# Two graph layers on one core: q kept on chip as fp16 pairs, one-hot matrices on DVE, unrolled gathers

## The chip, the cores and the metric

One core of a Trainium2 chip runs the whole program in one launch. The time is device microseconds of that core from start to end of the launch; a kernel's time is the median of its runs. TensorE is called PE, VectorE DVE, ScalarE ACT, GpSimd POOL and SyncE SP.

## The reference, cut to what matters

There are 6250 nodes of 512 features (fp32) and 100000 edges, sorted by destination.

```
# layer 0
h   = relu(layernorm(x))
agg = segment_sum(h[src], dst) / max(deg, 1)
g   = relu(agg @ W_l.T + b_l + h @ W_r.T)
x   = x + batchnorm(g)
# layer 1
h = relu(layernorm(x))
Q, K, V = h @ Wq, h @ Wk, h @ Wv                 # 8 heads of 64
score = exp(clip(sum(K[src] * Q[dst]) / 8, -5, 5))    # per edge and head
wV = segment_sum(V[src] * score, dst);  Z = segment_sum(score, dst)
out = x + batchnorm(h + wV / (Z + 1e-6))
```

## The kernel before, in words

The nodes are cut into 49 windows of 128. The sorted edges are cut into groups of 256 (two halves, G = 2, of 128 edges), and a table lists 440 steps, each one group against one window; a group that crosses a window's border appears in two steps. The tables stay in SBUF: `src_t` (source rows, an out-of-range number where the edge belongs to another window), `rel_t` (destination within the window), and small rows with one value a step: `col_t` (the window's column in `sums`), `par_t`, `new_t` (1 where a window begins), `row_t` and `qcol_t`. Stages follow one another with a barrier between them:

- `prepare` (L111) makes the tables. Its POOL part ends in eight gathers written out one after another (L179 to L183).
- `embed` (L565) makes y = h @ W_l.T for every window, stored as fp16 pairs in DRAM (`y_d`).
- `aggregate` (L829) does the 440 steps of layer 0. POOL gathers y rows of each half (L881, two gathers a step, eight steps of buffers, U = 8) with indices that ACT copies beforehand for pairs of steps from `src_t` into `idx` (L856, "staging", since the loop's step is a register). DVE makes a one-hot matrix of both halves in one instruction (L904). PE multiplies it with the gathered rows (L977).
- `dense` (L267, called with `layer` = 1 only) splits the three weight matrices into a high and a low part (L462 to L468 on ACT, L382 on DVE), and for each window makes Q, K and V with 36 matmuls (L549). K and V go to `kv_d`. Q, divided by 8, is stored as high and low part in fp32 slots to `q_d` (L329, L435, L492).
- `attend` (L1112) does the 440 steps of layer 1, each engine with its own order, several steps apart: PE does in its iteration t `total(t-2)`, `turn(t+2)`, `expand(t+1)`; ACT does `weigh(t-1)`, staging for every second step (L1212, L1213), `copy_hot(t+2)`; DVE does `multiply(t)`, `scale(t-1)`, `reduce(t)`, `one_hot(t+3)` of the second half on even steps only (L1266), a flush where a window ended (L1006, L1017), `clip(t)`. POOL makes the other one-hot halves (L1192: one half on even steps, both on odd ones) and then issues the step's two gathers of K and V rows (L1196, 512 KB each). SP loads the window's q at each new window from `q_d` into four slots (L1170). `expand` multiplies the turned one-hot (`hotT`) with q's two parts (L1341), so every edge has its q row in PSUM.
- the last two stages make batch norm and the output.

Within one engine everything runs in the written order; between engines semaphores count steps.

Of the kernel before, what the change touches and what calls it, by code (L numbers as in the profile page):

```python
# [16 lines left out]
F32 = mybir.dt.float32  # L17
# [14 lines left out]
def build(nc, x, src, dst, W_l, b_l, W_r, gamma0, beta0, Wq, Wk, Wv, gamma1, beta1, out):  # L32
# [21 lines left out]
    QB = 4  # L54
# [8 lines left out]
    q_d = nc.dram_tensor("q_d", (WINDOWS * P, 2 * D), F32).ap()  # L63
# [15 lines left out]
    with life:  # L79
# [4 lines left out]
        row_t = sb(life, "row_t", [1, TS], I16)  # L84
        qcol_t = sb(life, "qcol_t", [1, TS], I16)
# [25 lines left out]
        def prepare():  # L111
            with ExitStack() as ctx:
# [34 lines left out]
                def _(block):  # L147
# [63 lines left out]
                    def _(dve):  # L211
# [23 lines left out]
                        then(nc.vector.tensor_scalar(row_t[:, :], win[:, :], float(P), None, ALU.mult))  # L235
                        then(nc.vector.tensor_copy(win_t[:, :], win[:, :]))
                        then(nc.vector.tensor_copy(qcol_t[:, :], win[:, :]))
                        then(nc.vector.tensor_scalar(par_t[:, :], qcol_t[:, :], 1, None, ALU.bitwise_and))
                        then(nc.vector.tensor_scalar(par_t[:, :], par_t[:, :], float(D), None, ALU.mult))
                        then(nc.vector.memset(zero[:, :].bitcast(F32), 0.0))  # L240
                        then(nc.vector.tensor_scalar(qcol_t[:, :], qcol_t[:, :], QB - 1, None, ALU.bitwise_and))
                        then(nc.vector.tensor_scalar(qcol_t[:, :], qcol_t[:, :], float(2 * D), None, ALU.mult))
# [24 lines left out]
        def dense(layer, given, A_bc=None, C_bc=None):  # L267
# [3 lines left out]
            M = len(given)  # L271
            tag = str(layer)
            with ExitStack() as ctx:
                w_hi = sb(ctx, "w_hi" + tag, [P, M, KC, D], F32R)
                w_lo = sb(ctx, "w_lo" + tag, [P, M, KC, D], F32R)
                x_sb = sb(ctx, "x_sb" + tag, [P, 2, D])
                x1 = sb(ctx, "x1_sb", [P, 2, D]) if layer else x_sb
                h = sb(ctx, "h" + tag, [P, 2, D])
                st = sb(ctx, "st" + tag, [P, 6])
                mv = sb(ctx, "mv" + tag, [P, 2])  # L280
                sd = sb(ctx, "sd" + tag, [P, 1])
                rs = sb(ctx, "rs" + tag, [P, 2])
                nb = sb(ctx, "nb" + tag, [P, 2])
                hT_hi = sb(ctx, "hT_hi" + tag, [P, 2, D], F32R)
                hT_lo = sb(ctx, "hT_lo" + tag, [P, 2, D], F32R)
                o_sb = sb(ctx, "o_sb" + tag, [P, 2, 2, D])
                w_st = [o_sb[:, :, :, :].rearrange("p a b d -> p (a b) d")]
                if layer:
                    q_sb = sb(ctx, "q_sb", [P, 2, 2, D], F32R)
                    w_st.append(q_sb[:, :, :, :].rearrange("p a b d -> p (a b) d").bitcast(F32))  # L290
                else:
                    b_row = sb(ctx, "b_row", [1, D])
                    b_bc = sb(ctx, "b_bc", [P, D])
                ps_t = [pb(ctx, f"ps_t{tag}{k}", [P, 512]) for k in range(2)]
                ps_o = [[pb(ctx, f"ps_o{tag}{k}{j}", [P, 512]) for j in range(M)] for k in range(2)]

                w_in, w_turned, w_high, w_split, b_in = sems("w_in" + tag, M), *(
                    sem(n + tag) for n in ("w_turned", "w_high", "w_split", "b_in"))
                x_in, t_made, t_sum, normal = sems("x_in" + tag, 2), sem("t_made" + tag), sem("t_sum" + tag), sem("normal" + tag)
                var_ready, dev_ready, shift_ready, h_made = (sem(n + tag) for n in ("var_ready", "dev_ready", "shift_ready", "h_made"))  # L300
                q_high = sem("q_high" + tag)
                turned, high, split, made, by_act, by_dve = (
                    sem(n + tag) for n in ("turned", "high", "split", "made", "by_act", "by_dve"))
                kept, stored = sems("kept" + tag, 2), sems("stored" + tag, 2)

                def later(w):

                    return not isinstance(w, int) or w >= 2

                @nc_block()  # L310
                def _(block):
                    @block.sync
                    def _(sp):
                        def load(w, par, n=P):
                            if later(w):
                                sp.wait_ge(t_made if layer else h_made, w - 1)
                            sp.dma_start(x_sb[0:n, par, :], x[ds(w * P, n), :]).then_inc(x_in[par], 16)
# [6 lines left out]
                        def store(w, par):  # L324
                            sp.wait_ge(by_act, w + 1)
                            sp.wait_ge(by_dve, w + 1)
                            rows = ds(w * P, P)
                            if layer:
                                sp.dma_start(q_d[rows, :], q_sb[:, par, :, :].rearrange("p a d -> p (a d)").bitcast(F32)).then_inc(stored[par], 16)  # L329
                                sp.dma_start(kv_d[rows, :], o_sb[:, par, :, :].rearrange("p a d -> p (a d)")).then_inc(stored[par], 16)  # L330
                            else:
                                sp.dma_start(y_d[rows, :], o_sb[:, par, 0, :]).then_inc(stored[par], 16)
                                sp.dma_start(z_d[rows, :], o_sb[:, par, 1, :]).then_inc(stored[par], 16)

                        def both(w, par, n=P):
                            load(w + 3, 1 - par, n)
                            if layer:
                                keep(w + 1, 1 - par)
# [1223 lines left out]
```

## Time and profile before

| | us |
|---|---|
| median of 3 runs | 3829.07 (3824.32 to 3831.52) |
| the profiled execution | 3821.38 |
| its span | 3819.5 |
| PE busy | 3054.6 (80%) |
| DVE busy | 2468.3 (65%) |
| POOL busy | 2474.2 (65%) |
| ACT busy | 1706.6 (45%) |
| DMA, mean over the span | 210 GB/s |

Busy shares are averages over seven stages with different limits, so they say little by themselves; the stages have to be read one by one. Times of single instructions overlap a little (the next one begins before the end of the last is recorded), so the distance from start to start is what an instruction takes from its engine.

### The profile page before, as it was taken

To read this page: it belongs to the slowest core of one execution; us is meant where nothing else is said; L and a number is where in the kernel's file an instruction comes from. 1 tells how busy PE (TensorE), PEld (TensorE's weight loads), DVE (VectorE), ACT (ScalarE), POOL (GpSimd) and SP (SyncE) were. 2 spreads that over 40 slices of the span, in tenths; PEclk is the share of its full clock that TensorE was granted. 3 is DMA by queue.
4 is the path that set the end of the run, shared out by engine and by line. 5 is a ranking of instruction groups with operands and counts; after the bars stand their busy time and mean duration, and the time that the engine had idled before them with its cause. 6 is when DMAs were issued, how large, how long until landed. Compare 5 with 4: busy or idle time off the path is not lost. (4 is left out here: it accounts for less than half of the span.)

```text
span 3819.5 us, 67243 instructions
## 1 busy us (share of the span) xinstructions
PE 3054.6 (80%) x11640; PEld 1638.0 (43%) x11641; DVE 2468.3 (65%) x4394; ACT 1706.6 (45%) x6882; POOL 2474.2 (65%) x2589
## 2 busy tenths in 40 slices
PE   4776666777777774999989999999999999999740
PEld 2332222222222221788865555555555555555310
DVE  5443333333333334555559899989999989989999
ACT  2331000000000001222238888888888888888410
POOL 1005777777777774111138888888888888888555
PEclk9888777676666666999989999999999999999865
DMA  2334666666666664555558888888888888888447
GB/s 72 108 109 141 177 176 176 176 176 176 177 175 177 175 174 133 187 211 205 206 208 276 271 276 275 275 275 276 273 277 277 275 275 278 275 272 279 144 114 218
DMA packets 277576, 801.77 MB, mean 210 GB/s; under 512 B 55747, under 2 KB 55749, under 8 KB 277514
## 3 DMA queue, kind: packets, MB, share of 16 engines
q0 software_dynamic: 197504, 615.66, 51.4%
q1 hardware_dynamic: 73022, 172.98, 13.4%
q10 hardware_dynamic: 7020, 12.80, 0.9%
q8 instruction: 9, 0.15, 0.0%
q14 instruction: 21, 0.17, 0.0%
HBM read 981.14 MB, written 103.52 MB: 284 GB/s over the span
## 5 line engine op out<-in xcount | busy, mean ns | idle before, releaser
L881 POOL DMA_INDIRECT rows<-y_d,idx x880 | 898.2, 1021 | 556.1 <-DVE rows L894 288.5
L1229 ACT ACTIVATE kv<-kv,wgt 128x64 f32<-128x64 f32 x4400 | 1097.9, 334 | 0.0
L1196 POOL DMA_INDIRECT kv<-kv_d,idx x880 | 935.5, 1063 | 208.8 <-issue 197.5
L1353 PE MATMUL psa<-kv,hot 128*128 128x512 f32 x1760 | 870.3, 617 | 94.6 <-DVE parts L1281 41.0
L977 PE MATMUL pss<-rows,hot 128*128 128x512 f16 x1760 | 627.1, 491 | 284.3 <-DMA rows<-y_d,idx 246.0
L1273 DVE TENSOR_TENSOR kv<-kv,ps_q 128x1024 f32<-128x1024 f32 x440 | 535.3, 1217 | 138.9 <-DMA kv<-kv_d,idx 89.9
L856 ACT COPY idx<-src_t 128x4 int32 (+1 forms) x224 | 43.0, 193 | 1130.9 <-DMA rows<-y_d,idx 1127.7
L1286 DVE TENSOR_REDUCE score<-kv 128x16 f32<-128x1024 f32 x440 | 532.0, 1209 | 0.0
L1341 PE MATMUL ps_q<-q,hotT 128*128 x1760 | 521.9, 418 | 6.1 <-DVE kv L1273 2.0
L1353 PEld LDWEIGHTS psa<-kv,hot 128*128 128x128 f32 x1760 | 304.1, 190 | 446.2 <-issue 440.1
L1192 POOL TENSOR_SCALAR hot<-lane,rel 128x128 fp32r<-128x128 f32 x660 | 423.6, 653 | 46.5 <-DVE kv L1260 31.0
L911 DVE TENSOR_SCALAR rd<-psc 128x1 f32 (+1 forms) x49 | 7.7, 158 | 602.4 <-PE psc L979 602.4
L977 PEld LDWEIGHTS pss<-rows,hot 128*128 128x128 f16 x1760 | 126.1, 108 | 505.9 <-issue 458.8
L1341 PEld LDWEIGHTS ps_q<-q,hotT 128*128 128x128 f32 x1760 | 301.4, 191 | 52.4 <-issue 13.4
L371 POOL TENSOR_TENSOR x_sb<-x_sb,C_bc 128x512 f32<-128x512 f32 x49 | 63.2, 1290 | 397.9 <-DMA x_sb<-in_x 397.9
L904 DVE TENSOR_TENSOR hot<-lane,rel_t 128x256 f16<-128x256 f32 x440 | 188.0, 428 | 154.8 <-issue 104.9
L1358 PE MATMUL psw<-parts,hot 128*128 128x16 f32 x880 | 285.4, 396 | 0.0
L1279 DVE TENSOR_TENSOR kv<-kv,wgt 128x384 f32<-128x384 f32 x440 | 257.6, 586 | 0.3 <-ACT wgt L1222 0.3
L1358 PEld LDWEIGHTS psw<-parts,hot 128*128 128x128 f32 x880 | 163.7, 191 | 192.3 <-issue 190.4
L549 PE MATMUL ps_o<-w_hi,hT_hi 128*128 128x512 f32 x588 | 238.9, 406 | 0.0
L549 PE MATMUL ps_o<-w_hi,hT_lo 128*128 128x512 f32 x588 | 231.6, 394 | 0.0
L549 PE MATMUL ps_o<-w_lo,hT_hi 128*128 128x512 f32 x588 | 231.1, 393 | 0.0
(192 smaller groups left out, 3806.7 us busy)
## 6 DMA issues: line engine op xcount, KB each, us to landing
q<-q_d SPq DMA_DIRECT2D x440, 512.0 KB
q_d<-q_sb SPq DMA_DIRECT2D x49, 512.0 KB, 2.7
kv_d<-o_sb SPq DMA_DIRECT2D x49, 512.0 KB, 4.0
rows<-y_d,idx POOLq DMA_INDIRECT x880, 3.7
kv<-kv_d,idx POOLq DMA_INDIRECT x880, 5.3
y_d<-y SPq DMA_DIRECT2D x49, 256.0 KB, 2.0
x_d<-x_sb SPq DMA_DIRECT2D x49, 256.0 KB, 3.9
h_d<-h SPq DMA_DIRECT2D x49, 256.0 KB, 3.4
```

The source lines that it names most:

```text
L549: last = nc.tensor.matmul(ps_o[par][k][:, :], a, b[:, k, c, :], start=(c == 0 and j == 0), stop=(c == KC - 1 and j == 2))
L881: pool.indirect_dma_start(rows[:, u, g, :], None, y_d[0:N, :], bass.IndirectOffsetOnAxis(idx[:, u // H, k:k + 1], 0), bounds_check=limit, ...
L977: nc.tensor.matmul(pss[:, ds(par, D)], hot[:, u, g, :], rows[:, u, g, part * D:(part + 1) * D], start=False, stop=(g == G - 1 and part == ...
L1192: last = nc.gpsimd.tensor_scalar(hot[:, u, g, :], lane[:, :], rel[:, u // H, k + g:k + g + 1], None, ALU.is_equal)
L1196: pool.indirect_dma_start(kv[:, u, g, :], None, kv_d[0:N, :], bass.IndirectOffsetOnAxis(idx[:, u // H, k + g:k + g + 1], 0), bounds_check= ...
L1229: last = nc.scalar.mul(v, v, wgt[:, u, g * HEADS + h:g * HEADS + h + 1])
L1273: nc.vector.tensor_tensor(k, k, ps_q[u % 2][:, :].rearrange("p (g d) -> p g d", g=G), ALU.mult).then_inc(multiplied, 1)
L1279: nc.vector.tensor_tensor(v, v, w.unsqueeze(3).to_broadcast([P, G, HEADS - HA, DH]), ALU.mult)
L1286: nc.vector.tensor_reduce(score[:, u, :].rearrange("p (g h) -> p g h", g=G), kv[:, u, :, 0:D].rearrange("p g (h d) -> p g h d", h=HEADS), ...
L1341: last = nc.tensor.matmul(ps_q[u % 2][:, g * D:(g + 1) * D], hotT[:, u % 2, g * P:(g + 1) * P], q[:, ds(col + k * D, D)], start=(k == 0), ...
L1353: nc.tensor.matmul(pss[:, ds(par, D)], hot[:, u, g, :].bitcast(F32), kv[:, u, g, D:2 * D], start=False, stop=(g == G - 1), skip_group_chec ...
L1358: last = nc.tensor.matmul(psc[:, 0:2 * HEADS], hot[:, u, g, :], parts[:, u % 4, g, :, :].rearrange("p t h -> p (t h)"), start=False, stop= ...
```

## The change

Four things change. (1) q is no longer stored to DRAM and read back. `dense` writes it as two fp16 parts into the columns of `sums` that its window has just freed, and `expand` reads it there with an fp16 `hotT`. So that the low fp16 part keeps its bits, the columns of Wq are multiplied by a power of two derived from their norm and those of Wk by the inverse (with the 1/8); that takes four squares on ACT, four fp32 matmuls and five DVE instructions before the weights are split, and the loads of Wq and Wk are issued ahead of those of x. (2) In `attend` DVE makes the one-hot matrix of both halves in every step, and POOL makes none. (3) POOL's gathers in `aggregate` and `attend` are written out for all 440 steps and take their indices from `src_t`; ACT's staging is gone in both stages. (4) In `total` the opening of the counts moves into the branch that opens the window, so there is one branch in place of two; three small table rows are no longer made.

```diff
-                            if layer:
-                                sp.dma_start(q_d[rows, :], q_sb[:, par, :, :]....bitcast(F32)).then_inc(stored[par], 16)
...
+                        dve.wait_ge(w_normed, KC)
+                        nc.vector.tensor_scalar(norm2, ps_o[1][0][:, :].bitcast(I32), 0x7F000000, 1,
+                                                ALU.bitwise_and, ALU.logical_shift_right).then_inc(grown, 1)
+                        dve.wait_ge(grown, 1)
+                        nc.vector.tensor_scalar(grow[:, 0, :], norm2, -1.0, float(199 << 23), ALU.mult, ALU.add).then_inc(grown, 1)
+                        nc.vector.tensor_scalar(grow[:, 1, :], norm2, float(52 << 23), None, ALU.add).then_inc(grown, 1)
+                        dve.wait_ge(grown, 3)
+                        for k in range(2):
+                            dve.wait_ge(w_in[k], 16)
+                            nc.vector.tensor_tensor(w_st[k][:, :, :], w_st[k][:, :, :],
+                                                    grow[:, k, :].bitcast(F32).unsqueeze(1).to_broadcast([P, KC, D]),
+                                                    ALU.mult).then_inc(w_grown, 1)
...
+                            nc.scalar.activation(x1[:, c % 2, :], w_st[0][:, c, :], ACT.Square).then_inc(w_squared, 1)
...
+                            nc.tensor.matmul(ps_o[1][0][:, :], ones[:, :], x1[:, c % 2, :], start=(c == 0), stop=(c == KC - 1)).then_inc(w_normed, 1)
...
+                            nc.scalar.copy(q_part(w, 0), ps_o[par][0][:, :]).then_inc(q_high, 1)
+                            nc.vector.tensor_tensor(q_part(w, 1), ps_o[par][0][:, :], q_part(w, 0), ALU.subtract).then_inc(by_dve, 1)
...
-                            for g in range(1 + u % 2):
-                                last = nc.gpsimd.tensor_scalar(hot[:, u, g, :], lane[:, :], rel[:, u // H, k + g:k + g + 1], None,
-                                                               ALU.is_equal)
...
+                        for s in range(STEPS):
+                            u = s % U
...
+                            pool.wait_ge(ps_made, s + 1)
                             for g in range(G):
+                                m = s * G + g
                                 pool.indirect_dma_start(kv[:, u, g, :], None, kv_d[0:N, :],
-                                                        bass.IndirectOffsetOnAxis(idx[:, u // H, k + g:k + g + 1], 0),
+                                                        bass.IndirectOffsetOnAxis(src_t[:, m:m + 1], 0),
...
-                            nc.vector.tensor_scalar(hot[:, u, 1, :], lane[:, :], rel[:, u // H, (u % H) * G + 1:(u % H) * G + 2],
-                                                    None, ALU.is_equal).then_inc(hot_made_dve, 1)
+                            nc.vector.tensor_tensor(hot[:, u, :, :], lane[:, :].unsqueeze(1).to_broadcast([P, G, P]),
+                                                    rel_t[:, ds(s * G, G)].unsqueeze(2).to_broadcast([P, G, P]),
+                                                    ALU.is_equal).then_inc(hot_made, 1)
...
-                            pe.wait_ge(q_in[u % QB], 16 * (i * (U // QB) + u // QB + 1))
...
-                                                            q[:, ds(col + k * D, D)], start=(k == 0), stop=(k == 1))
+                                                            slots[:, ds(col * 2 + k * D, D)], start=(k == 0), stop=(k == 1))
```

## Rows read from the trace of the kernel before

**Rows 1.** Windows by stage: start:end, length, each engine's busy us, clock, DMA share, GB/s.
```profile
317.00:1486.00 1169.00, 849.56 (x3326) 323.51 (x3326) 389.07 (x833) 42.55 (x220) 898.16 (x880) 0.70 0.63 175
1534.00:1973.00 439.00, 433.19 (x1952) 350.46 (x1952) 225.48 (x475) 124.11 (x240) 58.15 (x45) 0.99 0.55 201
1988.00:3564.00 1576.00, 1477.76 (x5352) 834.56 (x5351) 1435.53 (x2508) 1380.09 (x6136) 1348.05 (x1529) 0.99 0.82 275
```
**Rows 2.** Groups of POOL, 1988 to 3564: line, shapes, count, busy, mean ns, idle before.
```profile
L1196 POOL DMA_INDIRECT kv<-kv_d,idx x874 | 927.7, 1061 | 207.4 <-issue 196.4 <-PE psw L1358 10.1 <-ACT idx L1213 0.9
L1192 POOL TENSOR_SCALAR hot<-lane,rel 128x128 fp32r<-128x128 f32 x655 | 420.5, 653 | 15.5
```
**Rows 3.** Groups of DVE, 1988 to 3564.
```profile
L1273 DVE TENSOR_TENSOR kv<-kv,ps_q 128x1024 f32<-128x1024 f32 x440 | 535.3, 1217 | 138.9 <-DMA kv<-kv_d,idx 89.9 <-PE ps_q L1341 44.0 <-issue 1.6
...
L1279 DVE TENSOR_TENSOR kv<-kv,wgt 128x384 f32<-128x384 f32 x438 | 256.5, 586 | 0.0
...
L1266 DVE TENSOR_SCALAR hot<-lane,rel 128x128 fp32r<-128x128 f32 x218 | 70.1, 322 | 0.0
L1017 DVE COPY sums<-psa x48 | 33.0, 688 | 0.0
```
**Rows 4.** Timeline of DVE, one step of attend: start us, us, instruction.
```profile
2824.60 0.46 DVE L1292 TENSOR_SCALAR score<-score 128x16 f32<-128x16 f32 x1
2824.70 1.22 DVE L1273 TENSOR_TENSOR kv<-kv,ps_q 128x1024 f32<-128x1024 f32 x1
2825.84 0.70 DVE L1279 TENSOR_TENSOR kv<-kv,wgt 128x384 f32<-128x384 f32 x1
...
2826.54 1.21 DVE L1286 TENSOR_REDUCE score<-kv 128x16 f32<-128x1024 f32 x1
2827.67 0.27 DVE L1266 TENSOR_SCALAR hot<-lane,rel 128x128 fp32r<-128x128 f32 x1
2827.86 0.44 DVE L1292 TENSOR_SCALAR score<-score 128x16 f32<-128x16 f32 x1
```
**Rows 5.** Timeline of PE's weight loads, one round of attend.
```profile
1998.25 0.41 PEld L1353 LDWEIGHTS psa<-kv,hot 128*128 128x128 f32 x2
...
2000.50 0.75 PEld L1341 LDWEIGHTS ps_q<-q,hotT 128*128 128x128 f32 x4
2001.30 0.43 PEld L1353 LDWEIGHTS psa<-kv,hot 128*128 128x128 f32 x2
```
**Rows 6.** Timeline of ACT, one round of attend.
```profile
2806.32 2.50 ACT L1229 ACTIVATE kv<-kv,wgt 128x64 f32<-128x64 f32 x10
...
2809.51 0.34 ACT L1229 ACTIVATE kv<-kv,wgt 128x64 f32<-128x64 f32 x1
```
**Rows 7.** Groups, 400 to 1400 (aggregate): gathers of POOL, one-hots of DVE.
```profile
L881 POOL DMA_INDIRECT rows<-y_d,idx x756 | 771.5, 1021 | 230.5 <-issue 206.7 <-PE psc L979 16.2 <-ACT idx L856 7.6
...
L904 DVE TENSOR_TENSOR hot<-lane,rel_t 128x256 f16<-128x256 f32 x377 | 161.4, 428 | 134.4 <-issue 92.4 <-PE psc L979 41.2
```
**Rows 8.** Timeline of POOL: a gather of the loop in aggregate.
```profile
809.60 1.00 POOL L881 DMA_INDIRECT rows<-y_d,idx  x1 [0.30 <-issue]
```
**Rows 9.** Timeline of POOL: a gather of the part written out, in prepare.
```profile
27.02 0.94 POOL L181 DMA_INDIRECT eidx<-src_pad,grp_col  x1 [0.30 <-issue]
```
**Rows 10.** DMA issues of the page: count, median us from issue to landing.
```profile
rows<-y_d,idx POOLq DMA_INDIRECT x880, 3.7
```
**Rows 11.** Timeline of all engines, the start of dense.
```profile
1512.31 2.18 ACT L468 CAST w_hi<-o_sb 128x512 fp32r<-128x512 f32 x4 [14.46 <-DMA o_sb<-in_L_gnn_Wq]
...
1515.48 0.37 SPq L348 DMA_DIRECT2D o_sb<-in_L_gnn_Wv  x1
...
1521.46 2.50 DVE L382 TENSOR_TENSOR w_lo<-o_sb,w_hi 128x512 fp32r<-128x512 f32 x4 [3.34 <-ACT w_hi L468]
```
**Rows 12.** Timeline of PE: an fp32 matmul of 512 columns outside the busy stages.
```profile
1492.54 1.91 PE L1074 MATMUL ps_s<-S,ones 128*128 128x512 f32 x2
```
**Rows 13.** Timeline of all engines, the start of attend: the first expand waits for q.
```profile
1985.37 2.07 PE L1341 MATMUL ps_q<-q,hotT 128*128 x4 [1.61 <-DMA q<-q_d]
```

More of the change, by code:

```diff
@@ L264, in _, with dense @@
                                                   ps_t[n % 2][:, 0:GE].rearrange("p (g s) -> p g s", g=G)).then_inc(stored, 1)
[L267 to L272 removed]
+        def dense(A_bc, C_bc):
+            M = 3
+            given = (Wq, Wk, Wv)
             with ExitStack() as ctx:
[L274 to L287, printed above, removed]
[L288 to L301 removed]
@@ L852, in _ @@
                 def _(block):
-                    @block.scalar
-                    def _(act):
-                        def stage(i, part):
-                            nc.scalar.copy(idx[:, part, :], src_t[:, ds((i * U + part * H) * G, H * G)]).then_inc(staged, 1)
-                        for part in range(U // H):
-                            stage(0, part)
-                        with act.Fori(0, ITERS) as i:
-                            for part in range(U // H):
-                                for u in range(part * H, part * H + H):
-                                    act.wait_ge(rows_in[u], (i + 1) * 16 * G)
-                                alone(act)
-                                stage(i + 1, part)
                     @block.gpsimd
@@ L1161, in times @@
                             at(ITERS, t - STEPS)
-                    @block.sync
-                    def _(sp):
-                        def fetch(i, u, regs):
-                            s, r = i * U + u, u % QB
-                            row, col, new = regs
-                            sp.wait_ge(expanded, s + 1)
-                            sp.dma_start(q[:, ds(col[u], 2 * D)].bitcast(F32), q_d[ds(row[u], P), :], cond=new[u]).then_inc(q_in[r], 16)
-                        with sp.Fori(0, ITERS) as i:
-                            regs = [load_values(mybir.EngineType.SP, table, i * U, U, most) for table, most in
-                                    ((row_t, (WINDOWS - 1) * P), (qcol_t, (QB - 1) * 2 * D), (new_t, 1))]
-                            for u in range(U):
-                                fetch(i, u, regs)
                     @block.gpsimd
@@ L1242, in at @@
                                 weigh(*step)
-                            if u % H == 0 and u and (not isinstance(i, int) or 0 <= i < ITERS):
-                                restage(i, u // H - 1)
-                            if u == 0 and (not isinstance(i, int) or 0 < i < ITERS):
-                                restage(i - 1, U // H - 1)
                             if step := steps(i, u, 2):
                                 copy_hot(*step)
-                        for part in range(U // H):
-                            stage(0, part)
                         for u in range(1, U, 2):
@@ L1305, in at @@
                                 reduce(*step)
-                            if (step := steps(i, u, 3)) and step[2] % 2 == 0:
+                            if step := steps(i, u, 3):
                                 one_hot(*step)
                             if step := steps(i, u, -1):
-                                flush(*step)
+                                flush_ended(*step)
                             if step := steps(i, u, 0):
```

293 lines of the change are left out of this document (112 added, 181 removed).

## Prediction

> **What bounds the kernel now.** I read the windows first, one for each stage [rows 1]. Three stages hold 3184 of the 3819.5 us of the span: aggregate 1169 us, dense 439 us, attend 1576 us. In dense PE is busy 433 of 439 us, so PE sets its pace. In the other two all engines look busy or none does, so the busy share doesn't say; the groups and their idle time do.
>
> In attend (440 steps, 1576 us, 3.58 us a step) POOL is busy for 1348 us, the lowest of the four. But its groups [rows 2] show that the rest is not waiting: 207.4 + 15.5 us of idle time, of which 196.4 us is "issue" (about 0.24 us ahead of each gather) and only 11 us waits for another engine. 1348 + 223 = 1571 us, the whole stage. POOL is the bound, with 2 x 1.061 us of gathers, 1.5 x 0.653 us of one-hots and 0.47 us of issue a step (3.57 us). DVE, in contrast, has 139 us in which it waits ahead of its multiply, 89.9 us of it for the gathered rows [rows 3]: the rows are late because POOL is. PE can do a round in 3.05 us (1998.25 to 2001.30, from one first weight load of `total` to the next [rows 5]) and ACT, with its staging, in 3.19 us (2806.32 to 2809.51 [rows 6]).
>
> In aggregate the groups show 1.021 us a gather and 230.5 us idle ahead of 756 of them [rows 7], 0.305 us each, nearly always the same 0.30 us [rows 8]. Together 1002 us in a window of 1000: POOL is the bound there too, with nothing but its gathers, 1.326 us each.
>
> **The change, part by part.**
>
> *POOL in attend.* 1.5 one-hots a step leave (655 x 0.653 = 420 us over the stage). What stays is 2 x (1.061 + 0.30) = 2.72 us. The value is not critical: anything under 3.3 us is hidden behind DVE.
>
> *DVE in attend takes the bound.* Its step, start to start from the timeline [rows 4]: multiply 1.14 (to 2825.84), scale and parts together 0.70 (to 2826.54), reduce 1.13, one-hot of one half 0.19, clip 0.10 (2824.60 to 2824.70). The scale shown is a long one: 0.70 us against a mean of 0.586 [rows 3], so I take 0.59 for scale and parts over the stage. Now a one-hot of 128x256 comes in every step. The same instruction with an fp16 result lasts 428 ns in aggregate, against 322 ns for the 128x128 one in attend [rows 3, 7]. Spans overstate the distance by 0.08 to 0.09 (1.22 against 1.14, 0.27 against 0.19 [rows 4]), so it takes 0.34 us. New step: 1.14 + 0.59 + 1.13 + 0.34 + 0.10 = 3.30 us. A flush adds 0.69 us and a small instruction 48 times [rows 3], 0.08 a step: 3.38 us. I add 0.04 for waits that even a saturated engine has and take 3.42 us. The lower end is 3.33 (no waits, and 0.05 less for the scale); the upper is 3.589, the distance of the multiplies today, if the waits for `ps_q` (44.0 us, 0.10 a step [rows 3]) and for rows stay as they are and only move. Gain: 439 x (3.589 - 3.42) = 74 us; between 0 and 114 us.
>
> What is behind the new one-hot: on DVE the clip of the same step, on which ACT's exp, then `total`, and so PE's `expand` of three steps later hang. That ring (clip, exp and two handovers about 0.7, ten muls 2.5 [rows 6], total and turn 2.25, expand 0.8 [rows 5], then multiply to clip 3.2) is about 9.5 us for three steps, 3.17 us each, so below DVE's 3.42.
>
> *fp16 q on PE.* Four f32 matmuls of `expand` take 0.80 us (2000.50 to 2001.30 [rows 5]), 0.20 for 512 columns at the full 2.4 GHz clock; fp16 can't be much below. The four cost between 0.1 us less and 0 a step, and PE is no bound. Nothing. The branch that goes and the two waits that go (q, second one-hot semaphore) are on the same engine: nothing.
>
> *ACT.* Staging leaves attend and aggregate. ACT goes below its 3.19 us, far from the bound. POOL's waits for it are 0.9 and 7.6 us of events with the usual 0.30 gap [rows 2, 7]: nothing.
>
> *Gathers written out, aggregate.* POOL-bound, so here every ns of a gather counts 880 times. The gap before a gather is 0.30 in the loop and 0.30 in the part written out in prepare, whose gather lasts 0.94 against 1.00 [rows 8, 9], but that one fetches other rows, with nothing beside it. I take 0 for the 1.326 us. Ends: 0.08 less (70 us gain), and the rival below.
>
> The Trainium skill bears on this ("Runtime: NRT & Kernel Launch", section "Instruction fetch mechanics"): straight code is streamed ahead and mostly hidden, while a taken branch out of the fetched part stalls. By it the loops would be what costs, and writing out would be free or better; the gaps of 0.30 in both forms show no such gain.
>
> *q traffic.* 49 stores and 49 loads of 512 KB leave. DMA is at 0.82 in attend and 0.55 in dense [rows 1], neither is a bound; the rows that DVE waits for are late by POOL's issue. In dense PE stays busy: nothing in the loop. At the end of dense one store less is waited for, about 1 us. At the start of attend the first `expand` waited 1.61 us for q [rows 13]; POOL's first gather also comes a one-hot earlier: 2 us.
>
> *Start of dense.* Before, Wq is there at 1512.3 and the last low part of Wv ends at 1524.0 [rows 11]. After: Wq is issued ahead of two loads of x, about 0.4 us each [rows 11], and there at 1511.5; a square takes 0.55 (as one of the four casts); four fp32 matmuls at the half clock of a resting PE, 1.84 each [rows 12], 7.4 us, to 1519.5; three DVE instructions of 512 elements 1.9 (0.57 each, half of the 1.14, and waits); two multiplies of 2048 elements, 2.2 each (twice the 1.14 of 1024), to 1525.8. ACT has begun with Wq meanwhile; the low parts of Wq end 2.5 us later, at 1528.3; Wv is issued only then and needs 6.0 to its first low part and 2.5 for the four, as before (1515.48, 1521.46): 1536.8. That is 12.7 us later, take 13 (8 to 18). Nothing hides it: PE waits for the last split.
>
> *The wait that DVE gets there* (for the norms) has the weight splits and the first statistics behind it; all of it is in the 13.
>
> Sum, against the profiled execution: 3821.4 + 13 - 1 - 2 - 74 + 0 = 3757 (the small table rows that go, under 2 us, are left out). The median of the runs is 7.7 us above that execution, so **3765 us**.
>
> **Rivals.** A measurement of this kernel tells a change from none at about 0.2%, 8 us.
>
> *A, the waits only move:* attend stays at 3.56. For it: DVE, PE and ACT are all over 3.05 us with three rings between them, and DVE still lost 44 us to `ps_q` while POOL had the blame. Against it: in stretches where the rows are there, steps with a one-hot run at 3.24 [rows 4]. 3829 + 10 - 439 x 0.03 = 3826 us.
>
> *B, the code written out stalls POOL (slower).* 1760 gathers have their own instructions, fetched by DMA beside gathers that fill 0.63 to 0.82 of the DMA engines. In attend POOL has 0.7 us a step to spare; in aggregate none. If every 16 gathers (the old loop body) cost one landing of 3.7 us [rows 10], that is 55 x 3.7 = 203 us: 3968 us. It decides from 17 such stalls on (64 us of gain divided by 3.7), one in 51 gathers. Against: eight written-out gathers with the same 0.30 gap [rows 9].
>
> *C, writing out makes the gather shorter* (the waits compare with a constant, no index copy is between): 880 x 0.06 = 53 us less, and up to 70 by the 0.94 + 0.30 of prepare [rows 9]: 3705 us.
>
> *D, attend falls to ACT's and PE's pace*, 3.2 us: -171 us in place of -74, 3668 us. That needs DVE to lose 0.2 us. The Trainium skill ("SBUF — State Buffer", section "Who interferes with whom") lets a POOL instruction block DVE's faster forms while it runs. By it the clip, 0.46 and 0.44 us for 16 elements in [rows 4], would shrink when POOL's one-hots go; but POOL's gathers stay, and the sum above holds the clip at 0.10 already.
>
> **Chances.** Forecast 0.58 (its own range 3735 to 3790), A 0.15, B 0.10, C 0.12, D 0.05. The range 3695 to 3830 leaves out B, D and bits of C and A. Faster by over 0.2%: forecast, C, D and a little of A, 0.79. Within 0.2%: most of A, 0.09. Slower: B and the end of A with a long start of dense, 0.12.
>
> **What would show it.** After, the groups of POOL in attend have some 250 us of idle time ahead of the gathers, released by PE's `total`, and DVE's idle time before its multiply falls from 139 to under 40 us; the multiplies are 3.42 us apart; the new one-hot lasts about 0.43 us, 440 times; aggregate keeps 1.32 to 1.33 us a gather and its 1167 us; dense's first product comes at about +13 us. It is wrong if the gathers of aggregate come at another distance, or if DVE in attend still waits over 100 us.

## The result, and the profile after

| | before | after |
|---|---|---|
| median of the runs, us | 3826.7 (4 runs) | 3740.67 (3739.14 to 3741.92, 4 runs) |
| the profiled execution, us | 3821.38 | 3740.36 |
| its span, us | 3819.5 | 3738.0 |

The ratio is 0.9776, with a 95% interval from 0.9759 to 0.9793: 86 us less, where 64 less had been forecast (3829 to 3765).

The page of the kernel after, busy time of the engines over the span:

```profile
PE 3025.4 (81%) x11648; PEld 1516.3 (41%) x11649; DVE 2503.8 (67%) x4615; ACT 1632.8 (44%) x6216; POOL 1991.4 (53%) x1929
```

POOL lost 483 us of work and DVE gained 36 us; neither number says what the time did. The stages do. Windows of the kernel after (start:end, length, busy us of PE, its weight loads, DVE, ACT and POOL, granted clock, DMA share, GB/s); the three stretches are aggregate, the products of dense, and attend from its first to its last multiply:

```profile
317.00:1486.00 1169.00, 858.77 (x3326) 325.55 (x3326) 390.29 (x834) 0.00 (x0) 897.82 (x880) 0.70 0.63 175
1545.00:1981.00 436.00, 433.69 (x1953) 350.68 (x1952) 236.00 (x475) 124.22 (x240) 58.40 (x46) 1.00 0.41 142
1996.00:3482.00 1486.00, 1430.14 (x5354) 708.74 (x5353) 1456.45 (x2727) 1347.22 (x5697) 868.80 (x873) 1.00 0.81 274
```

Against [rows 1]: aggregate has the same POOL time in a window of the same length, dense nearly the same length at a later place and with a lower DMA share (0.41 against 0.55), and attend has become 1486 us long, with DVE busy for 1456 of them. The groups of POOL and of DVE in attend answer to [rows 2] and [rows 3]:

```profile
L1080 POOL DMA_INDIRECT kv<-kv_d,src_t x873 | 868.9, 995 | 601.2 <-PE psw L1226 464.1 <-issue 137.1
```
```profile
L1132 DVE TENSOR_TENSOR kv<-kv,ps_q 128x1024 f32<-128x1024 f32 x440 | 533.0, 1211 | 32.6 <-PE ps_q L1207 24.0 <-issue 8.4
...
L1138 DVE TENSOR_TENSOR kv<-kv,wgt 128x384 f32<-128x384 f32 x438 | 239.8, 547 | 0.0
L1124 DVE TENSOR_TENSOR hot<-lane,rel_t 128x256 fp32r<-128x256 f32 x437 | 179.2, 410 | 0.0
L1151 DVE TENSOR_SCALAR score<-score 128x16 f32<-128x16 f32 x439 | 73.4, 167 | 0.1
```

POOL now waits 464 us for PE to free a buffer, where it waited for no more than 11 us before. (A gather that waits has its issue gap inside the wait. A step of two gathers needs 2 x 1.30 us from start to start, so what POOL really has to spare is 440 x (3.384 - 2.60), about 345 us.) DVE's idle time ahead of the multiply fell from 138.9 to 32.6 us, and no part of it is for the gathered rows any longer. The bound has moved from POOL to DVE. One step on DVE, to be laid beside [rows 4]:

```profile
2802.40 0.19 DVE L1151 TENSOR_SCALAR score<-score 128x16 f32<-128x16 f32 x1
2802.50 1.21 DVE L1132 TENSOR_TENSOR kv<-kv,ps_q 128x1024 f32<-128x1024 f32 x1
2803.63 0.54 DVE L1138 TENSOR_TENSOR kv<-kv,wgt 128x384 f32<-128x384 f32 x1
2804.10 0.16 DVE L1140 TENSOR_TENSOR parts<-wgt,parts 128x16 fp32r<-128x16 f32 x1
2804.19 1.20 DVE L1145 TENSOR_REDUCE score<-kv 128x16 f32<-128x1024 f32 x1
2805.32 0.40 DVE L1124 TENSOR_TENSOR hot<-lane,rel_t 128x256 fp32r<-128x256 f32 x1
2805.65 0.16 DVE L1151 TENSOR_SCALAR score<-score 128x16 f32<-128x16 f32 x1
2805.73 1.20 DVE L1132 TENSOR_TENSOR kv<-kv,ps_q 128x1024 f32<-128x1024 f32 x1
```

Start to start: multiply 1.13, scale 0.47, parts 0.09, reduce 1.13, one-hot of both halves 0.33, clip 0.08; 3.23 us without a gap.

Where the 81.5 us between the two spans come from, by the start of the same instruction in both traces:

| place | before | after | difference |
|---|---|---|---|
| first gather of aggregate | 317.4 | 316.8 | -0.6 |
| last gather of aggregate | 1482.5 | 1481.8 | -0.7 |
| first product of dense | 1534.0 | 1545.0 | +11.0 |
| last store of K and V issued | 1969.0 | 1980.1 | +11.1 |
| first multiply of attend | 1987.5 | 1996.1 | +8.5 |
| last multiply of attend | 3563.3 | 3481.6 | -81.7 |

The 439 distances between the multiplies fell from 3.589 to 3.384 us, 90 us in all. The start of dense gives 11 back. Nothing else moves by more than 3 us.

### The profile page after: what moved, and what is told of

Its sections match the earlier page's. It is cut to its first block and busy times, and to the rows that moved or that the text cites. A ratio compares the mean times of both kernels' runs of the same rounds, so it can differ in the third digit from the quotient of the medians.

```text
span 3738.0 us, 59649 instructions
## 1 busy us (share of the span) xinstructions
PE 3025.4 (81%) x11648; PEld 1516.3 (41%) x11649; DVE 2503.8 (67%) x4615; ACT 1632.8 (44%) x6216; POOL 1991.4 (53%) x1929
## 5 line engine op out<-in xcount | busy, mean ns | idle before, releaser
L1080 POOL DMA_INDIRECT kv<-kv_d,src_t x880 | 876.9, 997 | 633.4 <-PE psw L1226 464.1
L831 POOL DMA_INDIRECT rows<-y_d,src_t x880 | 898.0, 1020 | 555.8 <-DVE rows L838 288.1
L1132 DVE TENSOR_TENSOR kv<-kv,ps_q 128x1024 f32<-128x1024 f32 x440 | 533.0, 1211 | 32.6 <-PE ps_q L1207 24.0
L1207 PE MATMUL ps_q<-sums,hotT 128*128 x1760 | 454.4, 381 | 0.1
L1226 PE MATMUL psw<-parts,hot 128*128 128x16 f32 x880 | 302.2, 415 | 0.0
L1138 DVE TENSOR_TENSOR kv<-kv,wgt 128x384 f32<-128x384 f32 x440 | 240.9, 547 | 0.3 <-ACT wgt L1095 0.3
L1207 PEld LDWEIGHTS ps_q<-sums,hotT 128*128 128x128 f16 x1760 | 172.4, 98 | 110.5 <-issue 2.0
L1198 PE MATMUL ps_h<-ident,hot 128*128 128x128 f32 x880 | 193.3, 302 | 14.9 <-DVE hot L1124 14.4
```

Source lines behind the costliest of these rows:

```text
L831: pool.indirect_dma_start(rows[:, u, g, :], None, y_d[0:N, :], bass.IndirectOffsetOnAxis(src_t[:, m:m + 1], 0), bounds_check=limit, oob_is ...
L1080: pool.indirect_dma_start(kv[:, u, g, :], None, kv_d[0:N, :], bass.IndirectOffsetOnAxis(src_t[:, m:m + 1], 0), bounds_check=limit, oob_is_ ...
L1132: nc.vector.tensor_tensor(k, k, ps_q[u % 2][:, :].rearrange("p (g d) -> p g d", g=G), ALU.mult).then_inc(multiplied, 1)
L1138: nc.vector.tensor_tensor(v, v, w.unsqueeze(3).to_broadcast([P, G, HEADS - HA, DH]), ALU.mult)
L1198: last = nc.tensor.transpose(ps_h[:, g * P:(g + 1) * P], hot[:, u, g, :].bitcast(F32), ident[:, :])
L1207: last = nc.tensor.matmul(ps_q[u % 2][:, g * D:(g + 1) * D], hotT[:, u % 2, g * P:(g + 1) * P], slots[:, ds(col * 2 + k * D, D)], start=(k ...
```

## The experiments

All of them were timed against the kernel before on the same chip. The kernel after was not among them, so a run is laid beside it by the two ratios. "Step" is the distance of the multiplies in attend, first to last in the profiled execution, divided by 439.

| run | what | median us | step us |
|---|---|---|---|
| | before | 3824 to 3827 | 3.589 |
| | after | 3740.7 | 3.384 |
| e1_pool_hots | after, one-hots back on POOL | 3831.2 | 3.591 |
| e2_only_dve_hots | before, one-hots on DVE | 3728.9 | 3.368 |
| e4_hot_twice | after, DVE's one-hot twice | 3878.3 | 3.695 |
| e5_loops | after, gathers in loops, staging | 3744.6 | 3.390 |
| e7_q_traffic | after, q's transfers as ballast | 3740.9 | 3.382 |
| e10_wv_first | after, other order in dense | 3737.7 | 3.385 |
| e6_pool_spare_hot | after, POOL makes a spare half | 3745.3 | 3.394 |
| e3_half_pool | after, one half each | 3723.6 | 3.359 |
| e9_alternate | after, POOL one half of four | 3731.9 | 3.365 |
| e11_before_half | before, one half each | 3725.3 | 3.359 |
| e12_before_alternate | before, POOL one half of four | 3720.9 | 3.349 |

### Who the bound was, and who it is

**e1_pool_hots** undoes one part of the change. (Comments in the diffs here are put in for the reader.)

```diff
+                            for g in range(1 + u % 2):
+                                last = nc.gpsimd.tensor_scalar(hot[:, u, g, :], lane[:, :], rel_t[:, s * G + g:s * G + g + 1], None,
+                                                               ALU.is_equal)
...
-                            nc.vector.tensor_tensor(hot[:, u, :, :], ...       # every step
+                            nc.vector.tensor_tensor(hot[:, u, 1, :], ...       # even steps
```

> The changed kernel, but in attend POOL makes 1.5 one-hot halves a step again and DVE 0.5, as before; q stays on chip, gathers stay written out. Theory (POOL's one-hots were the bound, 2 gathers + 1.5 one-hots + issue = 3.57 us a step): multiplies 3.58 us apart again, DVE idle over 100 us ahead of the multiply, about 3828 us. Rival (the gain came from q's transfers, the fp16 matmuls or the unrolled gathers): 3.38 to 3.45 us apart, 3741 to 3765 us.

3831.2 us, ratio 1.0014 (1.0005 to 1.0024), step 3.591 us. The groups of POOL and DVE, from the first to the last multiply:

```profile
L1085 POOL DMA_INDIRECT kv<-kv_d,src_t x876 | 938.8, 1072 | 208.0 <-issue 208.0
L1080 POOL TENSOR_SCALAR hot<-lane,rel_t 128x128 fp32r<-128x128 f32 x656 | 411.2, 636 | 16.0
```
```profile
L1137 DVE TENSOR_TENSOR kv<-kv,ps_q 128x1024 f32<-128x1024 f32 x440 | 536.3, 1219 | 137.2 <-DMA kv<-kv_d,src_t 77.5 <-PE ps_q L1214 51.9 <-issue 5.0
```

POOL has no idle time but its issue gaps, and DVE is back at 77.5 us of waits for rows. With q on chip, fp16 matmuls and written-out gathers all in place, the whole gain of attend is gone. The rival falls.

**e2_only_dve_hots** does one part alone, in the kernel before. ACT's copy of `rel`, which no engine reads then, goes with it.

```diff
-                            for g in range(1 + u % 2):
-                                last = nc.gpsimd.tensor_scalar(hot[:, u, g, :], ...
...
-                            nc.vector.tensor_scalar(hot[:, u, 1, :], lane[:, :], rel[:, u // H, ...], None, ALU.is_equal)
+                            nc.vector.tensor_tensor(hot[:, u, :, :], lane[:, :]..., rel_t[:, ds(s * G, G)]..., ALU.is_equal)
```

> The kernel before with one part of the change alone: DVE makes both one-hot halves in every step; q still goes through DRAM in fp32 slots, gathers and index staging stay in loops. Theory: multiplies 3.39 to 3.42 us apart in place of 3.589, about 3826.7 - 439 x 0.18 = 3747 us, near the changed kernel, as the 11 us that its dense lost at its start are not paid here: perhaps 3740. Rival (q in DRAM or the staging hold the step up): 3.50 or more, over 3785 us.

3728.9 us, ratio 0.9752 (0.9736 to 0.9769), step 3.368 us: faster than expected, by 0.02 us a step and 11 us in all. The one part gives at least as much as the whole change. Its median is 12 us below that of the kernel after; the intervals of the two ratios overlap a little, the runs themselves (3726 to 3734 against 3739 to 3742) don't. In the profiled executions the way from the last gather of aggregate to the first multiply is 9.6 us shorter than in the kernel after, and attend itself 7.0 us. (Aggregate was 3.4 us longer in this execution. Nothing in it differs from the kernel before, where it took 1165.1 us; it varies like that.) Its DVE waits even less for PE (9.0 us against 24.0 us), although PE works with fp32 slots of q:

```profile
L1266 DVE TENSOR_TENSOR kv<-kv,ps_q 128x1024 f32<-128x1024 f32 x430 | 523.2, 1217 | 20.2 <-PE ps_q L1332 9.0 <-issue 8.4
```

**e4_hot_twice** makes DVE's share longer by a known amount.

```diff
+                            nc.vector.tensor_tensor(hot2[:, u, :, :], lane[:, :]..., rel_t[:, ds(s * G, G)]..., ALU.is_equal)
                             nc.vector.tensor_tensor(hot[:, u, :, :], lane[:, :]..., rel_t[:, ds(s * G, G)]..., ALU.is_equal).then_inc(hot_made, 1)
```

> The changed kernel with DVE's one-hot of 128x256 made twice in each step, the first time into a tile that nobody reads. Theory (DVE alone is the bound): the whole 0.332 us a step comes on top, 3.384 to 3.716 us, 3741 + 146 = 3887 us. Rival (the bound is a ring with slack on DVE): less than half of it, under 3814 us.

3878.3 us, ratio 1.0143 (1.0126 to 1.016), step 3.695 us: 0.311 us more for an instruction that takes 0.333 from start to start. The time grows by 137.6 us of 146, so 94% of the instruction arrives. A ring over three steps that runs through it once would show a third. So DVE alone is the bound after the change, and the ring over ACT and PE has slack at 3.38 us.

### The parts that were costed at nothing

**e5_loops** puts the gathers of both stages back into loops, with the staging by ACT as in the kernel before.

```diff
-                        for s in range(STEPS):
-                                                        bass.IndirectOffsetOnAxis(src_t[:, m:m + 1], 0),
+                        with pool.Fori(1, ITERS) as i:
+                                                        bass.IndirectOffsetOnAxis(idx[:, u // H, k:k + 1], 0),
```

> The changed kernel with POOL's gathers of both stages back in loops of eight steps, and ACT staging the indices for them. Theory (writing out is worth nothing: POOL's gap is 0.30 in either form, ACT has room): gathers of aggregate 1.326 us apart, multiplies of attend 3.38 us, 3737 to 3745 us. Rival (the written-out form shortens the gathers or frees ACT for the ring): over 3755 us.

3744.6 us (3744.3 to 3747.6), ratio 0.9795 (0.9779 to 0.9811), against 0.9776 of the kernel after: 4 us more, inside what was expected, and the intervals overlap. The group of the gathers in aggregate, in loops here and written out in the kernel after:

```profile
L849 POOL DMA_INDIRECT rows<-y_d,idx x880 | 898.1, 1021 | 559.1 <-DVE rows L862 291.4 <-issue 238.7 <-PE psc L947 20.4
```
```profile
L831 POOL DMA_INDIRECT rows<-y_d,src_t x880 | 898.0, 1020 | 555.8 <-DVE rows L838 288.1 <-issue 261.6 <-PE psc L923 6.1
```

1.021 and 1.020 us a gather. From the first to the last gather, aggregate takes 1165.1 us here; the written-out form took between 1163.9 and 1170.6 us in the eight executions that have it, so a difference under some 3 us is not to be read from one pair. In attend the loop form waits 313 us for ACT's staging where the written-out form waits for PE; it is POOL's spare time in both.

**e7_q_traffic** puts the bytes back and nothing else.

```diff
+                            sp.dma_start(q_d[ds(w * P, P), :], o_sb[:, par, :, :]...).then_inc(stored[par], 16)
...
+                        for i in range(WINDOWS):
+                            sp.wait_ge(expanded, AHEAD + i * U + 1)
+                            sp.dma_start(q[:, :], q_d[ds(i * P, P), :]).then_inc(q_in, 16)
```

> The changed kernel with q's transfers put back as ballast: a second store of 512 KB a window in dense and 49 loads of 512 KB in attend, that nobody reads. Theory (no stage is bound by DMA): attend 3.38 us a step, 3739 to 3746 us, the excess at the end of dense. Rival (the transfers cost the gathers time): over 3755 us.

3740.9 us, ratio 0.9781 (0.9765 to 0.9797). A window of 1480 us inside attend shows DMA at 0.85 and 292 GB/s. The step is the same, 3.382 us:

```profile
2000.00:3480.00 1480.00, 1423.50 (x5338) 705.49 (x5336) 1452.08 (x2720) 1343.51 (x5680) 871.19 (x873) 1.00 0.85 292
```

q's 50 MB cost nothing in attend. From the last gather of aggregate to the first multiply, with dense between them, this execution took 1.3 us more than that of the kernel after.

**e10_wv_first** shortens the start of dense by another order of the three weights.

```diff
-                        for k in range(2):                       # loads: Wq, Wk, then Wv into Wq's buffer
+                        for k in (0, 2):                         # loads: Wq, Wv, then Wk into Wv's buffer
...
+                        for c in range(KC):                      # Wv is split ahead of the wait for the norms
+                            part_low(c, w_st[2][:, c, :], w_lo[:, 2, c, :], w_hi[:, 2, c, :], w_high, w_split)
                         dve.wait_ge(w_normed, KC)
```

> The changed kernel with another order at the start of dense: Wq and Wv are loaded first, Wv is split while PE computes the norms, Wk comes into Wv's buffer and is scaled last. Theory (nothing hides the start of dense, PE waits for the last split, at 1535.0 in the changed kernel): the last low part ends 3 to 5 us sooner and the kernel takes 3736 to 3738 us. Rival (the start is hidden behind the statistics or the loads of x): 3741 us.

3737.7 us (3737.1 to 3738.8, 5 runs), ratio 0.9773 (0.976 to 0.9786). The last low parts end 2.6 us sooner, at 1532.4 against 1535.0, although Wq was issued 1.4 us later in this execution (1506.2 against 1504.7); counted from there it is 4.0 us, inside the 3 to 5 expected. The medians differ by 3.0. The timeline of e10, then that of the kernel after (start, length, and the gap before it with what ended it):

```profile
1529.92 2.50 DVE L362 TENSOR_TENSOR w_lo<-w_b,w_hi 128x512 fp32r<-128x512 f32 x4 [0.68 <-ACT w_hi L451]
```
```profile
1532.53 2.50 DVE L362 TENSOR_TENSOR w_lo<-o_sb,w_hi 128x512 fp32r<-128x512 f32 x4 [3.76 <-ACT w_hi L450]
```

The start of dense is on the path, with nothing to hide it. 3 us is at the edge of what the intervals can tell; the trace is the better witness here.

### POOL's spare time

After the change POOL has about 345 us to spare. Five runs try to give it work.

**e6_pool_spare_hot** gives it work that nobody needs.

```diff
+                            for g in range(1):
+                                last = nc.gpsimd.tensor_scalar(hot2[:, u, :], lane[:, :], rel_t[:, s * G + g:s * G + g + 1], None, ALU.is_equal)
```

> The changed kernel, and POOL makes one more one-hot half in each step into a tile that nobody reads; DVE still makes both that count. POOL then needs about 3.31 us a step, still less than DVE. Theory (a POOL compute instruction lengthens DVE's instructions that read SBUF twice: the scale went from 0.505 to 0.469 us when they left): scale at 0.50, 0.02 to 0.06 us a step more, 3750 to 3768 us. Rival (POOL and DVE don't touch, the scale was shorter for another reason): 3737 to 3745 us, scale 0.47.

3745.3 us, ratio 0.9795 (0.9779 to 0.9812), scale 0.470 us from start to start. That is the rival's scale, and a time at the upper edge of the rival's. Of DVE's instructions only the one-hot became clearly longer (0.348 against 0.332). But the run does not refute the theory, because it hardly tests it: only 32 of the 438 scales ran beside a POOL one-hot here (0.487 us, against 0.469 for the others). The traces at hand settle it. In the kernel before, 222 scales ran beside a POOL one-hot and took 0.539 us, the 216 others 0.470; the mean of the two is the 0.505 that the kernel before had. In e3 (next), 419 of 438 ran beside one, and the mean is 0.505 again. So the scale is short after the change because POOL's one-hots no longer meet it. It works both ways: POOL one-hots that began under a scale took 0.718 us in the kernel before, those that began under the reduce 0.632; in e6 381 of 440 began under the reduce, and took 0.623.

**e3_half_pool** gives it the first half of every step.

```diff
+                            for g in range(1):
+                                last = nc.gpsimd.tensor_scalar(hot[:, u, g, :], ...
+                            last.then_inc(hot_made_pool, 1)
...
+                            nc.vector.tensor_tensor(hot[:, u, 1, :], lane[:, :], rel_t[:, ds(s * G + 1, 1)]..., ALU.is_equal)
```

> The changed kernel, but POOL makes the first one-hot half of every step and DVE the second. Theory (DVE is the bound now at 3.38 us, POOL has about 0.78 us a step to spare): DVE loses 0.332 and gets about 0.20, 3.25 us; POOL 2 x 1.30 + 0.65 = 3.25 us; multiplies about 3.28 apart, 3741 - 439 x 0.10 = 3695 us. Rival 1 (the ring over ACT, PE and DVE holds the step): no change, 3741 us. Rival 2 (POOL's one-hots block DVE at the shared port): over 3.35, 3725 us or more.

3723.6 us, ratio 0.9735 (0.9719 to 0.9752), step 3.359 us. It gains 17 us, not the 46 of the theory. The step is the one of rival 2 (over 3.35), the time 1.4 us below it:

```profile
L1085 POOL DMA_INDIRECT kv<-kv_d,src_t x875 | 919.3, 1051 | 208.4 <-issue 208.4
L1080 POOL TENSOR_SCALAR hot<-lane,rel_t 128x128 fp32r<-128x128 f32 x437 | 323.7, 741 | 15.8
```
```profile
L1143 DVE TENSOR_TENSOR kv<-kv,wgt 128x384 f32<-128x384 f32 x415 | 242.6, 585 | 0.0
...
L1156 DVE TENSOR_SCALAR score<-score 128x16 f32<-128x16 f32 x416 | 111.3, 268 | 0.0
```

POOL again has nothing but issue gaps: 2 x 1.051 + 0.741 + 0.51 of idle time = 3.35 us a step, the step itself. So POOL is the bound, since its one-hot lasts 0.741 us here and 0.63 in e1 and e6, and DVE's scale (585 ns against 547) and clip (268 against 167) are longer too. The two slow each other, by how much depends on which of their instructions meet, and in e3 nearly every POOL one-hot meets the scale.

**e9_alternate** (in the kernel after), **e11_before_half** and **e12_before_alternate** (in the kernel before) try two splits. Shown is e12; e9 makes the odd half with a tensor_tensor and counts POOL's half on a semaphore of its own.

```diff
 # e12_before_alternate, e9_alternate
+                            if u % 2:
+                                nc.gpsimd.tensor_scalar(hot[:, u, 0, :], ...).then_inc(hot_made, 1)
...
+                            if u % 2 == 0:
+                                nc.vector.tensor_tensor(hot[:, u, :, :], ...
+                            else:
+                                nc.vector.tensor_scalar(hot[:, u, 1, :], ...
 # e11_before_half
-                            for g in range(1 + u % 2):
+                            for g in range(1):
...
-                            if (step := steps(i, u, 3)) and step[2] % 2 == 0:
+                            if step := steps(i, u, 3):
                                 one_hot(*step)
```

> The kernel before, with q in DRAM and all loops, where DVE makes both one-hot halves on even steps and on odd steps POOL makes the first and DVE the second. Theory: POOL needs 2.75 + 0.5 x 0.8 = 3.1 us, DVE's one-hot falls from 0.332 to 0.265 us on average, half of the contention of one POOL one-hot a step comes back: 3.32 to 3.34 us apart, 3.368 measured with all on DVE; 3709 to 3720 us. Rival (DVE no longer the bound, or contention eats it): 3729 us or more.

> The changed kernel with the split of the alternating run: DVE both halves on even steps, POOL one and DVE one on odd steps. Theory: the step of 3.349 us measured with q in DRAM, plus the 0.016 us by which the changed kernel's step was longer than its loop form with DVE alone: 3.36 us, 3728 to 3734 us. Rival (with PE shortened by fp16 there is more to win here): under 3722 us.

> The kernel before with the smallest edit: POOL makes the first half in every step (1.5 before), DVE the second in every step (0.5 before), both from the staged table, all else as before. Theory: POOL needs 2 x 1.055 + 0.47 + 0.70 = 3.28 us and up to 3.36 where it meets DVE (3.359 in the changed kernel with the same split); 3.33 to 3.37 us a step, 3712 to 3730 us. Rival (without q on chip this split does not hold): over 3745 us.

e12: 3720.9 us, ratio 0.9735 (0.9719 to 0.9751), step 3.349, both just outside what was expected (3.32 to 3.34, 3709 to 3720 us). e9: 3731.9 us, ratio 0.9759 (0.9746 to 0.9772), step 3.365. e11: 3725.3 us, ratio 0.974 (0.9727 to 0.9753), step 3.359. All three medians are below that of the kernel after, but e9's interval overlaps that of the kernel after (0.9759 to 0.9793); e12, e11 and e3 are level within their intervals. In e11 DVE's one-hot of one half is recorded with 385 ns (216 from start to start) and its clip with 269:

```profile
L1266 DVE TENSOR_SCALAR hot<-lane,rel 128x128 fp32r<-128x128 f32 x431 | 165.8, 385 | 0.0
L1292 DVE TENSOR_SCALAR score<-score 128x16 f32<-128x16 f32 x431 | 115.8, 269 | 0.0
```

The lowest median is that of the kernel before with nothing but the one-hots moved, most of them to DVE (e12): about 20 us, or 0.5%, less than the kernel after. It isn't clearly better than e3 or e11.

## Why the prediction was right

The time was inside the range and faster as forecast, with the mechanism as forecast: POOL the bound of attend before, DVE after. By its steps:

- *POOL in attend*: shown by e1. The step returns to 3.591 us with POOL's one-hots alone. The sign looked for, some 250 us of waits for `total`, was too small: 464 us, as the sum counted 2.72 us for two gathers where 2.60 would do, and a wait takes in the issue gap. The gathers fell from 1.061 to 0.995 us, which had not been foreseen and is hidden.
- *DVE's new step*: 3.384 us against 3.42. The mis-sized term is scale and parts: 0.59 in the sum, 0.469 + 0.085 = 0.554 in the trace. The 0.59 is the mean of the kernel before, half of whose scales met a POOL one-hot; the ones that met none took 0.470 there already (see e6). The one-hot was right (0.34 against 0.332). The clip and the waits after it came to 0.163 where 0.10 + 0.04 had been set. Together 90 us of gain in place of 74, which is 16 of the 22 us by which the forecast was too cautious. The rest is the start of dense (2) and the reference: the forecast leaned on a median of 3829 from three runs, while the four that the result was measured with have 3826.7, which is 5.3 us above the profiled execution, while the kernel after's median is 0.3 us above its own.
- *That DVE alone is the bound, and the ring is not*: shown by e4, 94% of an added instruction arrives.
- *fp16 q on PE, q's traffic, the staging, the written-out gathers, all costed at nothing*: q's traffic is shown by e7, staging and gathers by e5; for fp16 on PE, e2 shows that the step is no longer without it. The four weight loads of `expand` take 0.64 us in place of 0.75, a little more than had been allowed, and it helps nobody.
- *The merged branch, costed at nothing as well*: it moved a wait ahead of four matmuls, which the prediction didn't see. DVE waits 17.4 us behind these openings, against 4.1 in e2 (last section); no run undoes this part by itself.
- *Start of dense*: 13 us forecast, 11.0 measured, shown on the path by e10. The squares and matmuls had been taken too long (the norms were there at 1517.9, against 1519.5 in the sum; Wq came at 1510.9 in place of 1511.5), and the last low part ended at 1535.0 in place of 1536.8; the order of the steps is as written. The timeline of the kernel after, which ends with the row of the low parts at 1532.53 shown under e10:

```profile
1504.72 0.40 SPq L327 DMA_DIRECT2D o_sb<-in_L_gnn_Wq  x1
...
1511.61 6.29 PE L498 MATMUL ps_o<-x_sb,ones 128*128 128x512 f32 x8 [13.36 <-ACT x_sb L443]
...
1517.94 0.69 DVE L365 TENSOR_SCALAR x_sb<-ps_o 128x512 int32<-128x512 int32 x1 [13.72 <-PE ps_o L498]
...
1521.79 2.18 ACT L450 CAST w_hi<-o_sb 128x512 fp32r<-128x512 f32 x4 [5.73 <-DVE o_sb L373]
...
1526.40 0.38 SPq L331 DMA_DIRECT2D o_sb<-in_L_gnn_Wv  x1
```

- *Aggregate*: 880 gathers, 1165.1 us from the first to the last before and 1165.0 after (the two lie closer than executions of one form do, see e5). The gap of 0.30 us [rows 8] stays in the code written out for 440 steps:

```profile
1481.82 0.99 POOL L831 DMA_INDIRECT rows<-y_d,src_t  x1 [0.30 <-issue]
```

Of the rivals, A (the waits only move) fell with the 32.6 us of idle time on DVE. B (stalls of written-out code) and C (shorter gathers) fell with the equal distances. D had its direction right and its size wrong: the stage can't go below DVE's 3.23 us plus flushes. The note from the Trainium skill in D ("SBUF — State Buffer", section "Who interferes with whom"), on POOL instructions that block DVE's faster forms, agrees in part: the clip went from 278 to 167 ns (mean) as POOL's one-hots left, but stayed at 166 in e6, with a POOL one-hot in each step. The sum had held the clip at 0.10, the distance of the one in [rows 4]. Over the stage, without waits, it took 0.189 us from start to start before and 0.096 after. So 0.10 came out, but nothing in the sum said why the long clips would go; that this term is right is in part luck.

The Trainium skill's rule on instruction fetch ("Runtime: NRT & Kernel Launch", section "Instruction fetch mechanics") said that straight code is mostly hidden; the trace agrees, 0.30 us in either form. That loops would cost something does not show: 1.021 against 1.020 us. The prediction read the page too widely there: it has a stall only where a branch leaves the fetched part, and a round of aggregate's loop has 30 recorded POOL instructions, 16 of them gathers, in the trace of the kernel before. No run here shows a branch that leaves the fetched part.

## What to carry to other kernels

An engine that the busy table shows at 86% can be the one that sets the pace: add its issue gaps and look whether any of its idle time is a wait. When work is moved off it, the new time is the sum of start-to-start distances on the engine that takes the work, and that sum was good to 1%. Take the lengths of its instructions from steps in which the other engine is not beside it. And test each part of a bundled change by itself: here one part gave 98 us alone, and the rest of the bundle took 12 back, 11 of it at the start of dense.

## What was not expected of the hardware

**A clip that ends with a gather.** In e3 a DVE instruction of 16 elements (0.16 us alone) that starts while POOL's first gather after a one-hot is running ends with that gather. DVE's clips and POOL's gathers of the same stretch:

```profile
2803.12 0.44 DVE L1156 TENSOR_SCALAR score<-score 128x16 f32<-128x16 f32 x1
...
2806.38 0.45 DVE L1156 TENSOR_SCALAR score<-score 128x16 f32<-128x16 f32 x1
```
```profile
2802.51 1.08 POOL L1085 DMA_INDIRECT kv<-kv_d,src_t  x1 [0.17 <-issue]
...
2805.77 1.08 POOL L1085 DMA_INDIRECT kv<-kv_d,src_t  x1 [0.17 <-issue]
```

2803.12 + 0.44 = 2803.56 against 2802.51 + 1.08 = 2803.59, and 2806.83 against 2806.85. Of 250 clips of e3 that start under such a gather, 249 end within 0.05 us of its end; so do 102 of 142 in the kernel before, where rows 4 show two of 0.46 and 0.44 us. The gather that follows another gather does not do that in e3 (0 of 47), but it does in e9 (132 of 211), so it is not the one-hot ahead of it that matters. In e6, where POOL also makes a one-hot ahead of each pair, only 13 of 113 do, and the clip stays at 0.166 us. What tells e3 from e6 is where in the gather the clip starts. In e3 all 250 start over 0.5 us after the gather; in e6 the 13 do, and the other 100 start sooner. Of all 1413 clips of the thirteen traces that start in the first 0.5 us of a gather, 2 end with it. A late start is not enough by itself: of 50 in e4 that start between 0.5 and 0.8 us in, 10 do. The Trainium skill ("SBUF — State Buffer", section "Who interferes with whom") has a pair of ports that one of the two engines holds for a whole instruction when DVE is in a mode that uses both; that fits the late starts of e3 and not the early ones of e6. What POOL does in the two parts of a gather, no run here shows.

**In the kernel before, a gather after a one-hot is 1.08 us long with a gap of 0.17, one after a gather 0.99 with 0.30 (medians).** The sum is nearly the same, 1.25 and 1.29, so what looks like a shorter gather after the change is mostly the same time booked elsewhere.

**fp16 for q bought no time in attend.** With DVE as the bound, the step is 3.384 us with fp16 q on chip and 3.368 with fp32 slots from DRAM (e2). DVE waits 24.0 us for PE in the first and 9.0 in the second.

**The merged branch has put a wait ahead of four matmuls.** Most of those 15 us come from another part of the change, part (4). In the kernel before and in e2, `total` makes its four matmuls into `psa` first and waits for the next step's clip only then, to open the counts (`psw<-zero`). With the opening of the counts moved into the branch that opens the window, that wait stands ahead of the four. One opening of the kernel after, with the multiply that comes late, and one of e2:

```profile
2335.30 0.49 PE L1216 MATMUL psa<-zero 1*128 1x512 f32 x1
2336.27 0.27 PE L1218 MATMUL psw<-zero 1*128 1x16 f32 x1 [0.48 <-DVE score L1151]
2336.47 1.98 PE L1223 MATMUL psa<-kv,hot 128*128 128x512 f32 x4
...
2339.77 1.22 DVE L1132 TENSOR_TENSOR kv<-kv,ps_q 128x1024 f32<-128x1024 f32 x1 [0.33 <-PE ps_q L1207]
```
```profile
2329.45 0.49 PE L993 MATMUL psa<-zero 1*128 1x512 f32 x1
2329.87 1.98 PE L1344 MATMUL psa<-kv,hot 128*128 128x512 f32 x4
2331.79 0.27 PE L998 MATMUL psw<-zero 1*128 1x16 f32 x1
```

The groups of attend, after and e2:

```profile
L1218 PE MATMUL psw<-zero 1*128 1x16 f32 x49 | 13.5, 275 | 27.8 <-DVE score L1151 27.8
```
```profile
L998 PE MATMUL psw<-zero 1*128 1x16 f32 x49 | 13.3, 272 | 0.0
```

PE stands idle for 27.8 us there, and DVE's multiply after each of the 48 later openings comes late, 17.4 us in all against 4.1 in e2. PE's idle time at this place is 0.0 us in all four traces of kernels that have two branches (before, e2, e11, e12) and 17.8 to 60.0 us in all nine that have the merged one. No run moves the wait back and changes nothing else, so what that would give is an estimate from these waits, up to 13 us.
